# Two-layer attention, FFN and routed LoRA kernel: routing inputs formed in one VectorE operation, late z work over three engines, products without use in TensorE's waits

## The reference, cut to what matters

```python
crucial_features = crucial_channels * x
subcrucial_features = subcrucial_channels * x
c_max = jnp.max(crucial_features, axis=1, keepdims=True)
c_avg = jnp.mean(crucial_features, axis=1, keepdims=True) * (C / k)
...
A_S1 = _norm_active(_conv1d(crucial_x, conv_w), bn_gamma, bn_beta)
A_S2 = _norm_active(_conv1d(subcrucial_x, conv_w), bn_gamma, bn_beta)
return crucial_features * A_S1 + subcrucial_features * A_S2
...
logits = flat @ router_w.T + router_b
probs = jax.nn.softmax(logits, axis=-1)
topv, topi = jax.lax.top_k(probs, TOP_K)
gates = topv / jnp.sum(topv, axis=-1, keepdims=True)
h = jnp.einsum('nd,erd->ner', flat, A)
hw = h * w[:, :, None]
out = jnp.einsum('ner,eor->no', hw, Bm) * SCALING
```

## Time and profile before

| what | value |
|---|---|
| median of three runs | 1059.33 us (1059.22 to 1059.71) |
| profiled execution, span | 1059.44 us, 1057.7 us |
| PE, PE weight loads, DVE, ACT, POOL busy | 94%, 79%, 66%, 49%, 45% of the span |
| mean TensorE clock granted | 0.979 |
| DMA | 87.71 MB, 83 GB/s |

### The profile page before, as it was taken

The page is one execution under the profiler, slowest core; times in us unless marked ns, Lnnn a source line. Parts: engine busy times, 40 slices in busy tenths (PEclk is TensorE's granted clock), DMA queues, the critical chain, the costliest instruction groups (busy, mean ns, idle before and its releaser), DMA issues.

```text
span 1057.7 us, 18220 instructions
## 1 busy us (share of the span) xinstructions
PE 990.2 (94%) x5987; PEld 838.8 (79%) x6004; DVE 693.1 (66%) x1826; ACT 513.0 (49%) x1329; POOL 471.5 (45%) x367
## 2 busy tenths in 40 slices
PE   5999999999999999999999999999999999968475
PEld 4888888888888888888888888887887888844253
DVE  5566566656577776778655575566567657589755
ACT  4455444444444545454543544356355535556661
POOL 4554444444444554434434334426344444317441
PEclk9999999999999999999999999999999999989768
DMA  6422333333333222334322222212222221100002
GB/s 219 162 90 90 91 92 95 96 97 98 98 99 98 84 77 91 100 105 138 113 85 76 74 71 88 62 57 86 85 75 64 85 86 51 38 21 1 1 1 80
DMA packets 50412, 87.71 MB, mean 83 GB/s; under 512 B 6368, under 2 KB 15200, under 8 KB 50336
## 3 DMA queue, kind: packets, MB, share of 16 engines
q1 hardware_dynamic: 50336, 86.76, 26.6%
HBM read 84.64 MB, written 2.10 MB: 82 GB/s over the span
## 4 chain that ended last, share of the span: by engine, by line
PE 78%; DVE 6%; issue 6%; POOL 4%; ACT 2%; DVEq 2%; DMA 1%; SPq 0%; ACTq 0%; POOLq 0%
PE pX L1742 15%; PE pX L1744 15%; PE pX L1743 15%; PE pT L1994 5%; PE oacc L1742 5%; PE oacc L1743 5%; PE oacc L1744 5%; PE pS L1926 5%; PE pS L1747 2%; POOL wv_lo L571 1%; PE pT L1915 1%; PE pX L1859 1%; PE pX L1915 1%; POOL up L685 1%; DMA raw_k<-in_wk 1%
## 5 line engine op out<-in xcount | busy, mean ns | idle before, releaser
L571 POOL TENSOR_TENSOR wq_lo<-raw_q,wq_hi 128x512 fp32r<-128x512 f32 x64 | 82.7, 1292 | 264.0 <-DVE prob L1388 257.8
L1742 PE MATMUL pX<-wv_lo,cT_hi 128*128 128x256 f32 x512 | 149.4, 292 | 0.2 <-ACT q_sb L742 0.2
L870 ACT ACTIVATE prob<-score,neg_max 128x128 f32<-128x128 f32 x256 | 99.8, 391 | 97.4 <-DVE neg_max L1374 97.4
L1371 DVE TENSOR_TENSOR score<-pS,b_mask 128x512 f32<-128x512 f32 x64 | 44.2, 691 | 156.8 <-PE pS L1926 144.7
L1743 PE MATMUL pX<-wv_hi,cT_lo 128*128 128x256 f32 x512 | 144.1, 281 | 0.0
L1744 PE MATMUL pX<-wv_hi,cT_hi 128*128 128x256 f32 x512 | 144.0, 281 | 0.0
L571 POOL TENSOR_TENSOR wv_lo<-raw_v,wv_hi 128x1024 fp32r<-128x1024 f32 x32 | 77.1, 2410 | 121.9 <-ACT wv_hi L742 121.9
L742 ACT ACTIVATE v_sb<-pX 128x512 f32<-128x512 f32 x64 | 38.2, 597 | 163.7 <-PE pX L1744 163.7
L1742 PE MATMUL pX<-xT_lo,wq_hi 128*128 128x512 f32 x252 | 104.3, 414 | 5.7 <-POOL wq_lo L571 5.0
L1742 PE MATMUL oacc<-wo_lo,aT_hi 128*128 128x512 f32 x256 | 100.7, 393 | 3.5 <-DVE aT_lo L1354 2.5
L1742 PE MATMUL pX<-cT_lo,wk_hi 128*128 128x512 f32 x252 | 102.8, 408 | 0.0
(11 more groups left out here) (313 smaller groups left out, 2365.8 us busy)
## 6 DMA issues: line engine op xcount, KB each, us to landing
raw_k<-in_wk SPq DMA_DIRECT2D x64, 256.0 KB, 2.9
raw_q<-in_wq SPq DMA_DIRECT2D x64, 256.0 KB, 3.6
raw_v<-in_wv SPq DMA_DIRECT2D x32, 512.0 KB, 4.3
raw_o<-in_wo SPq DMA_DIRECT2D x64, 256.0 KB, 2.7
b_raw<-in_bias SPq DMA_DIRECT2D x64, 64.0 KB, 2.8
g_raw<-in_w_gate SPq DMA_DIRECT2D x16, 172.0 KB
g_raw<-in_w_up SPq DMA_DIRECT2D x16, 172.0 KB
f_raw<-in_w_down SPq DMA_DIRECT2D x4, 688.0 KB, 4.0
```

Source lines behind the costliest of these rows:

```text
L571: g.tensor_tensor(w_lo[c][:], w_raw[c][:], w_hi[c][:].bitcast(F32), ALU.subtract).then_inc(s_w_lo[c], 1)
L870: e = a.activation(prob[:, b, :], score[:, b, :], ACT.Exp, bias=neg_max[:, b:b + 1], accum_out=row_sum[:, b:b + 1])
L1371: v.tensor_tensor(score[:], pS[:].rearrange("p (b s) -> p b s", b=HB), b_mask[:], ALU.add).then_inc(s_scored, 1)
L1742: mm(dst, lh, rl, start=start, stop=False, skip_group_check=lint)
```

## The change

The residual branch of the third layer is written in another form: with z = (x - mean)/std, x + z*c is (c + std)*z + mean. So `gated` computes xr = (coef + sigma)*z in one operation on VectorE (`sigma` is the reciprocal of 1/std), GpSimd's addition is gone, and the token's mean is added at the end with the LoRA result. 1/std of the fourth layer is applied behind the router (to logits in `top_logits`, and with the factor 8/R in `rs_half`), for four tokens at once. A token's four coefficient pieces are computed by ScalarE (two), VectorE and GpSimd (one each); token 0's by VectorE (three) and ScalarE. All eight tokens are gated before the first choice of experts is finished, and the lora products stand behind the last router. For the four early tokens ScalarE adds the mean, and VectorE (0, 1) or GpSimd (2, 3) the residual. The ACT table for Exp is loaded behind the first five coefficient pieces.

For the late tokens, the split of k = 2 goes from VectorE to GpSimd, and its `add_down` from GpSimd to VectorE; both maxima of a token are one operation; the mean of the remaining part is total less crucial part, where TensorE computes the total (`z_totals`). In TensorE's program stand 65 products `keep_busy` (bf16, 128x512) whose results nothing reads. `z_shift(0)`, `z_out(0)`, `z_transposes(0)` and `residual_of(1)` move a little.

```diff
             z_rstd(1)
-            add_down(2)
             branches(0)
             z_rstd(2)
             branches(1)
             z_rstd(3)
+            branches(2)
...
-
-            for t in range(B):
-                pool.wait_ge(s_zc, t + 1)
-                g.tensor_tensor(xr[:, t, :], zc[:, t % 2, :], xr[:, t, :], ALU.add).then_inc(s_x3, 1)
-                if t >= 1:
-                    routed_rstd(t - 1)
-            routed_rstd(B - 1)
+            def one_coef(t):
+
+                g.tensor_scalar(coef[:, t, KT - 1, :], top[:, t // HB, KT - 1, t % HB, :], dA[:, KT - 1, t:t + 1],
+                                other[:, KT - 1, t:t + 1], ALU.mult, ALU.add).then_inc(s_coef_pool, 1)
+
+            def routed_rstd(i):
+                pool.wait_ge(s_x3_var, i + 1)
+                g.tensor_tensor(rs3[:, i * HB:(i + 1) * HB, 0], ve3[:, i * HB:(i + 1) * HB], neg_half[:, 0:HB],
+                                ALU.pow).then_inc(s_x3_rstd, 1)
+
+            pool.wait_ge(s_coef_dve, 1)
+            one_coef(1)
+            one_coef(2)
+            for t in range(3, B):
+                pool.wait_ge(s_x3, t - 2)
+                one_coef(t)
+            routed_rstd(0)
+            routed_rstd(1)
+            for t in (2, 3):
+                pool.wait_ge(s_lora_sb, t + 1)
+                pool.wait_ge(s_x4_done, 2)
+                g.tensor_tensor(xr[:, t, :], lora_sb[t], xr[:, t, :], ALU.add).then_inc(s_x4_pool, 1)
...
+                if k < 3:
...
+                    act.wait_ge(s_split_dve, 1)
+                for lt in range(KT):
+                    last = a.activation(sum_junk[:, 0, lt, :], split[k % 2][:, 0, lt, :], ACT.Copy,
...
+
+                act.wait_ge(s_l_proj, t + 1)
+                a.activation(lora_sb[t], l_bank[t % 2], ACT.Identity, bias=e_zmv[:, t, 0:1]).then_inc(s_lora_sb, 1)
...
+            weights_of(0, (3,))
+            weights_of(1, (0, 1))
+            weights_of(2, (0, 1))
+            a.activation(exp_again[:], ident[:, 0:1], ACT.Exp)
+            routed_out(0)
+            weights_of(3, (0, 1))
+            for t in range(HB):
+                routed_out(t + 1)
                 routed_heads(t)
-            lora_out(HB - 1)
+                weights_of(t + 4, (0, 1))
+            routed_out(5)
+            routed_heads(4)
+            routed_out(6)
+            routed_heads(5)
+            route_exp(0)
+            routed_out(7)
+            routed_heads(6)
+            routed_heads(7)
+            lora_in(0)
+            lora_in(1)
+            lora_out(0)
+            lora_in(2)
+            lora_out(1)
+            lora_in(3)
             route_exp(1)
+            lora_out(2)
+            lora_out(3)
             for t in range(HB, B):
-                lora_out(t)
+                lora_in(t)
 
         @block.vector
         def _(dve):
...
+            def rest_means():
+
+                dve.wait_ge(s_summed, B)
+                dve.wait_ge(s_z_total, HB)
+                v.scalar_tensor_tensor(out=stat[1][:, :, 1, HB:B], in0=stat[1][:, :, 0, HB:B], scalar=-CRUCIAL / REST,
+                                       in1=pA[:, 1040:1040 + HB * KT].rearrange("p (b k) -> p k b", k=KT),
+                                       op0=ALU.mult, op1=ALU.add).then_inc(s_maxed, 1)
...
             def gated(t):
 
                 dve.wait_ge(s_c_trans, t + 1)
-                if t >= 2:
-                    dve.wait_ge(s_x3, t - 1)
-                v.tensor_tensor(zc[:, t % 2, :], c_bank[t % 2][:], z[:, t, :], ALU.mult).then_inc(s_zc, 1)
+                v.scalar_tensor_tensor(out=xr[:, t, :], in0=c_bank[t % 2][:], scalar=sigma[:, t:t + 1],
+                                       in1=z[:, t, :], op0=ALU.add, op1=ALU.mult).then_inc(s_x3, 1)
...
+            def variances_of(i):
+
+                dve.drain()
+                for t in range(i * HB, (i + 1) * HB):
+                    v.bn_aggr(mv3[:, t, :], st3[:, t, :])
+                dve.drain()
+                v.tensor_scalar(ve3[:, group(i)], mv3[:, group(i), 1], EPS, None, ALU.add).then_inc(s_x3_var, 1)
...
+            def top_logits(i):
+
                 dve.wait_ge(s_rh, (i + 1) * HB)
-                v.tensor_tensor(prb[:, group, 0:E], rh[:, group, 0:E], rb[:].to_broadcast([P, HB, E]), ALU.add)
+                dve.wait_ge(s_x3_rstd, i + 1)
+                v.tensor_tensor(prb[:, group(i), 0:E], rh[:, group(i), 0:E],
...
-                v.tensor_tensor(hw[:, t, :, :], rh[:, t, E:E + ER].rearrange("p (e r) -> p e r", e=E),
-                                wexp[:, t, :, :].to_broadcast([P, E, R]), ALU.mult).then_inc(s_hw, 1)
+                v.scalar_tensor_tensor(out=hw[:, t, :, :], in0=rh[:, t, E:E + ER].rearrange("p (e r) -> p e r", e=E),
+                                       scalar=r_inv[:, t, 0:1], in1=wexp[:, t, :, :].to_broadcast([P, E, R]),
+                                       op0=ALU.mult, op1=ALU.mult).then_inc(s_hw, 1)
...
+                v.tensor_tensor(xr[:, t, :], lora_sb[t], xr[:, t, :], ALU.add).then_inc(s_x4_done, 1)
...
-                v.scalar_tensor_tensor(out=xr[:, t, :], in0=l_bank[t % 2], scalar=8.0 / R,
-                                       in1=xr[:, t, :], op0=ALU.mult, op1=ALU.add).then_inc(s_x4_done, 1)
-
+                v.scalar_tensor_tensor(out=xr[:, t, :], in0=l_bank[t % 2], scalar=mean_of(t),
...
+            weights_of(0, (0, 1, 2))
+            weights_of(1, (2,))
+            weights_of(2, (2,))
...
             gated(0)
             gated(1)
-            for t in range(HB):
+            for t in range(HB + 1):
+                if t + 3 < B:
+                    weights_of(t + 3, (2,))
+                dve.drain()
                 routed_stats(t)
-                gated(t + 2)
-            routed_stats(4)
-            route(0)
-            for t in range(HB):
-                weighed(t)
-            gated(6)
+                if t == HB - 1:
...
+            def keep_busy(bank, n):
+
+                for i in range(n):
+                    mm(bank, ident_b[:], w_rowT[0][:, 0, 0:512], start=True, stop=True)
...
+                for kt in range(KT):
+                    last = mm(pA[:, 1040 + k * KT + kt:1041 + k * KT + kt], z[:, HB + k, kt * P:(kt + 1) * P],
+                              rest_part[:], start=True, stop=True)
...
+            keep_busy(pZ[:], 11)
             token_transposes(0)
+            keep_busy(pZ[:], 3)
...
+            keep_busy(f_bank[:, 0:512], 1)
             for i in range(2):
                 pe.wait_ge(s_csum, i + 1)
                 mm(pA[:, 512 * (i + 1):512 * (i + 1) + 2], ones[:], csum[:], start=True, stop=True)\
                     .then_inc(s_ctotal, 1)
+                keep_busy(f_bank[:, 0:512], (5, 14)[i])
...
             coef_transposes(0)
             coef_transposes(1)
-            for t in range(HB):
-                routed_transposes(t)
-                coef_transposes(t + 2)
+            routed_transposes(0)
+            coef_transposes(2)
+            for t in range(B - 1):
+                routed_transposes(t + 1)
+                if t == 0:
+                    pe.wait_ge(s_ra, 1)
                 router(t)
...
+                hidden_transpose(t + 1)
                 lora(t)
-                if t + 2 < B:
-                    hidden_transpose(t + 2)
+                lora(t + 1)
 
 
 def kernel(**inputs):
```

More of the change, by code:

```diff
@@ L1070, in routed_heads @@
                 act.wait_ge(s_r_proj, t + 1)
[L1071 to L1073 removed]
+                copy(rh[:, t, :], pA[:, 0:E + ER]).then_inc(s_rh, 1)
             def route_exp(i):
```

235 lines of the change are left out of this document (127 added, 108 removed).

## The result

| kernel | median us (range, runs) | profiled run, span us |
|---|---|---|
| before | 1059.39 (1059.22 to 1059.71, 4) | 1059.44, 1057.7 |
| change | 1047.47 (1046.50 to 1048.79, 4) | 1046.50, 1044.8 |

The ratio of the two is 0.9881, 95% interval 0.9869 to 0.9893: 11.9 us faster, where 13.3 were forecast from the first three runs of before (1046.0 us, range 1042.5 to 1050.5). The runs of the change lie 2.3 us apart, those of before 0.5, and the profiled run is the shortest of the four: its trace gains 12.9, about 1.0 more than the median.

The account below looks back on a forecast made before the run. In the last 73 us no engine is full, so the chain of short steps between engines and TensorE's clock bound it. Terms -3.5 -0.9 -1.8 -6.9 -0.1 -1.4 +1.3 = -13.3 gave 1046.0 us, range 1042.5 to 1050.5.

Parts of the forecast that it names:

- gate and down products: Fillers ahead of gate and third down products keep full clock, but VectorE is later: 0, gate part between -0.3 and +0.4.
- late branches, to the convolution's end: Late tokens: add moved to VectorE, a split to GpSimd, convolution at full clock, ending at 1003.0: -3.5 us.
- totals and coefficients: Behind the convolution: two totals at full clock, fewer coefficient pieces on VectorE, coefficients at 1008.8 instead of 1013.2: -0.9 us.
- first token: Coefficients to first router: full-clock transposes, no GpSimd addition, against a later Exp table load; router at 1012.15: -1.8 us.
- routing loop: TensorE sets a 2.1 us period and all eight tokens are gated first, the last at 1022.3: -6.9 us.
- last gated token to last weights: VectorE's statistics, routings, weighed tokens, aggregations and a wait for GpSimd's power sum to 11.7 against 11.9: -0.1 us.
- the end: Last weights to last addition: final products at full clock, 6.4 us instead of 7.8: -1.4 us.
- outputs: After the last addition: GpSimd's additions hold SyncE's row, five outputs share the queue: +1.3 us, between 0 and 2.
- The forecast case: The whole kernel: all booked steps come true, 13.3 us saved, 1046.0 us; chance 0.46.
- 1.00 in every stretch: Sign for the forecast: clock 1.00 in every stretch from 941 to 1026 where before it was 0.50.
- Low clock at the end: Rival: clock falls behind the last router, three or four pairs cost 0.85 more each, 1049 us; chance 0.22.
- The case with products at 1.2 GHz on the path: Rival: clock down for all of 990 to 1008, fillers delay the path: +5.1, 1064.5 us; chance 0.03.

Follow-up runs that it names:

- experiment 1: The change without its 65 filler products, all else kept: 1049.56 us, ratio 0.9903 to the kernel before.
- (2): The kernel before with only the 65 filler products added at the same places of TensorE's program: 1055.68 us, ratio 0.9965.
- (7): The change with choice and weighing of tokens 0 to 3 put back between gated tokens 5 and 6, new operations kept: 1051.29 us, ratio 0.9909.
- experiment 3: The change with the late tokens' 128x1 z shifts written with a scalar column instead of two SBUF tensors: 1044.66 us, ratio 0.9856.
- experiment 6: The change with GpSimd's late additions of tokens 2 and 3 no longer waiting for VectorE's second x4 addition: 1048.42 us, ratio 0.9894.
- 12: Kernel of (11) with last statistics and variances ahead of the first two weighed tokens, ScalarE's exponential ahead of its second lora output: 1045.48 us, ratio 0.9862.
- (11): The change with scalar-column z shifts, outputs sent in order of readiness, and 7 instead of 14 products behind the second total: 1042.92 us, ratio 0.9837.
- experiment 4: The change with the addition of late token 2 back on GpSimd, ahead of the first split: 1047.79 us, ratio 0.9885.
- 9: The change without the 14 filler products ahead of the gate products, the other 51 kept: 1047.53 us, ratio 0.9876.
- 8: The change with six more filler products behind the first z transposes: 1048.63 us, ratio 0.9885.
- 10: The change with 7 instead of 14 filler products behind the second column total: 1047.96 us, ratio 0.9883.

## Why the prediction was right, and where its steps were not

| step | booked | in the traces |
|---|---|---|
| gate and down products | 0 | -0.9 (980.32 to 979.41) |
| late branches, to the convolution's end | -3.5 | -0.8 (1006.56 to 1004.88, less the 0.9) |
| totals and coefficients | -0.9 | -0.2 (1013.22 to 1011.32) |
| first token | -1.8 | -2.1 |
| routing loop | -6.9 | -8.2 (17.1 to 8.9 from first router to last gated token) |
| last gated token to last weights | -0.1 | -0.7 |
| the end | -1.4 | -1.5 |
| outputs | +1.3 | +1.4 |
| sum | -13.3 | -12.9 in the profiled run, -11.9 by the medians |

The forecast case came true: clock at 1.00 in the loop and at the end, a shorter period, all eight tokens gated ahead of the choice, outputs bunched. New order and operations are the larger part, as booked: without any product without use they give 10.3 (experiment 1); the products alone give 3.7 to the kernel before (2), and 2.3 to the changed one (1). Of the order, the place of the first choice is worth 3.0 (7). In the loop, from first router to last gated token, it is 17.1 before, 13.1 with the new operations in the old order (7) and 8.9 in the change. How the rest divides between ScalarE's fewer pieces and the addition that left GpSimd no experiment separates.

Three sums of the prediction are off by 0.1 to 0.2: four periods, a router and transposes are 9.9 and not 10.1, the terms of the end add up to 6.3 and not 6.4, and 11.9 less 11.7 is 0.2. Right sums would have given 13.7, inside the same range.

**The late branches: 0.8 instead of 3.5, and the step failed, not only its size.** What came is the convolution at full clock (1.51 instead of 2.77). The work ahead of it, booked 2.0 shorter, was 0.6 longer (23.9 instead of 23.3 from the multiplication at 979.41 to the last means at 1003.30). The step says that maxima and statistics follow "about 1.6 earlier" because the addition costs 1.13 on VectorE in place of a wait of 1.27. It took 1.79, and the two shifts near it 1.23 and 1.10 in place of 0.15. The last variance, expected at 994.2, came at 996.05, later than before (995.65). I had read the earlier trace rows with its 1.13 "beside a busy GpSimd" as the full price. The rule behind it is that a VectorE operation with two inputs in SBUF waits until GpSimd's running operation is over: experiment 3 shows it by taking one input away (0.21), experiment 6 by adding a GpSimd operation (0.16 to 0.73). The addition itself fits: it ended 0.55 behind GpSimd's operation each time, before (1.13) and in the change (1.79 and 1.13), so its duration only tells how early it began. The Trainium skill, "SBUF — State Buffer", section "Who interferes with whom", states it: a VectorE instruction with two SBUF inputs contends with a GpSimd one that reads SBUF, and the shared ports are an exclusive lock; these traces agree, to the 0.02 us at which the ends match. A small operation is not spared: 128x1 paid as much as 1.23. With the shifts mended the forecast holds: on the change's time the last variance of experiment 3 is at 993.1, the forecast's 994.2 less the 0.9 of the stage ahead is 993.3. The step also took the move of the third split to GpSimd as free; the last z, held by that split, took 0.45 longer than before. The clock is a small part: the prediction wanted 1.00 in every stretch, and 994 to 997 stood at 0.50, where eight products took 3.05 instead of 1.89 and delayed the last z transposes by about 0.3. With the shifts mended the clock held up to the convolution in two traces (3, 12) and fell at 998 in another (11), so that fall is only partly explained.

**Totals and coefficients: 0.2 instead of 0.9.** The two totals save 0.42 (0.38 each instead of 0.59) and the first coefficients 0.16; 0.36 went in an idle 0.43 of VectorE ahead of the line that squares the centred sums, for which the profile shows nothing that it waited for (0.07 before). It stands in every trace of the changed kernel and its variants but that of experiment 4 (0.07), and its cause stays open.

**Routing loop: 8.2 instead of 6.9.** TensorE sets the pace, as said, but at 1.80 and not 2.1: a router 1.09 and two groups of transposes 0.60 each follow one another without idle time, and overlap. My 2.1 was before's period less its waits, with the overlap left out.

**Gate stage: 0.9 for nothing booked.** Some 0.26 of it stands ahead of every edit (939.56 against 939.82 for the first statistics). The other 0.65 comes either way: the distance from there, 40.50 before, is 39.91 with the new order and no products (experiment 1, and 9 without the first 14), and 39.89 with the products and the old order (2). It is largely GpSimd again. Before, the multiplication of the third late token by a scalar column began 0.42 behind one of GpSimd's and took

```profile
952.59 1.13 DVE L1490 TENSOR_SCALAR t_y<-t_y,t_yinv 128x512 f32<-128x512 f32 x1
```

1.13; in the change it begins at 951.78, ahead of GpSimd's (952.20), and takes 0.49. An idle time of 0.47 ahead of its maximum is gone too (0.10); against both, a 128x2 operation with one tensor and constants at 954.90 took 0.71 instead of 0.17 and ended with GpSimd's operation.

**The rivals.** Low clock at the end did not occur in the change, nor without any of the products (1); in experiment 12 it came behind 2.00 us in which TensorE was idle (then 1.72 and 1.91 a pair). The case with products at 1.2 GHz on the path, which I priced at 1064.5 for the whole of 990 to 1008, exists on a small scale: in the traces of experiments 4, 7 and 8 the 14 products delay the first coefficient transposes by 1.1 us, and the 5 ahead of them the second total by 0.5. That the longer runs of the change (1047.35 to 1048.79) are such runs fits their lower mean clock, 0.997 to 0.992 against 0.998, but no trace of them exists. What makes the clock fall in one execution and not in the next is open.

## What to carry to other kernels

Before an operation is moved beside a busy GpSimd, count the SBUF tensors it reads on VectorE: with two it waits for GpSimd's running operation, however small it is itself. A form with a scalar column avoided that at 128x1 (0.21 against 1.23 us) but not at 128x512 (0.99 and 1.13 against 0.54 and 0.49 alone), so look at the ends of both engines' operations in the trace. Products that only keep TensorE's clock up should end well before the work behind them is ready at either clock, since they are paid twice when the clock has fallen; check them at 0.39 each and not at 0.21. Compare traces by distances from a point ahead of every edit, since their starts differ by up to 1.5 us. And a wait that the profile shows on the path may be cheaper than the order that removes it, if TensorE then idles ahead of work on the path.

## What the runs showed of the hardware that was not expected

- 128x1 on VectorE took 1.23 and 1.10 us with two SBUF tensors beside a running GpSimd operation, 0.15 and 0.16 without, 0.21 in the scalar-column form beside it. Other operations with one tensor did wait: 128x512 with a scalar column took 1.13 instead of 0.49, with two of them 0.99 instead of 0.54, and 128x2 with constants alone 0.71 instead of 0.17.
- It goes both ways: GpSimd's 128x512 addition, begun 0.4 behind a VectorE multiplication of two SBUF tensors (128x1376), took 2.34 (before) and 2.35 (change) instead of 1.27.
- The clock fell to 0.50 at 994 with TensorE busy 2.99 of the 4 us before, and at 1005 in five of the traces (experiments 4, 7, 8, 9, 10), behind 1000 to 1003 with 2.27 to 3.00 of 3 us busy; it held there in the change with 2.17 and in experiment 6 with 3.00.
- GpSimd's power of four columns took 1.04, of one column 0.55; its 128x128 coefficient piece with two scalar columns 0.59 at its first place.
- Eight outputs of 256 KB issued within 5.7 us landed 2.0 to 2.9 us after their issue, where one alone took 2.0.
